# A graph network with residual layer norm on one core: where listed rows get their node numbers, their x and z rows, and how chunk additions are cut

## The chip, the core and the metric

One NeuronCore of a Trainium2 chip runs the whole kernel in one launch. Its engines are TensorE (PE), VectorE (DVE), ScalarE (ACT), GpSimd (POOL) and SyncE (SP). The metric is device time in microseconds (us); less is better.

## What is computed

There are 50,000 nodes with 128 features and 25,000 edges, sorted by target node. Four edge convolutions follow one another; each takes the features of an edge's source (all earlier outputs joined) and 16 edge features, and takes the mean at the target:

```python
def _edge_conv(x, src, dst, edge_attr, W, b, denom):
    msg = jnp.concatenate([x[src], edge_attr], axis=1) @ W + b
    s = jax.ops.segment_sum(msg, dst, num_segments=x.shape[0])
    return s / denom[:, None]
h = _edge_conv(x, src, dst, edge_attr, W0, b0, denom)
outputs = [h]
for W, b in ((W1, b1), (W2, b2), (W3, b3)):
    cat = jnp.concatenate(outputs, axis=1)
    outputs.append(_edge_conv(cat, src, dst, edge_attr, W, b, denom))
return _layernorm(x + outputs[-1])
```

The targets are drawn with a squared uniform number, so low node numbers have many edges.

## The kernel before

**Front.** Up to about 300 us POOL gathers x rows of all edges, PE sums them by target into UT in SBUF, and DVE makes tables of the edges by one-hot matmuls.

**Products.** Then 36 groups of 512 summed rows (18 steps of two) go through PE (products with M and WE), ACT (scaling into HS3, two buffers), SP (stores three parts of each row to part_rows) and POOL (L686, adds the fourth part as z to the node's row of x_and_z_of_nodes). While they run, DVE and PE make lists in `list_work(g)`, one piece for each group g: the edges whose source is itself a target (the first list, up to 70 blocks of 128), the edges among those that are needed once more (the second list), and their targets. `list_work(34)` calls `lists_done`, whose last step is eight calls in `unit_counts` (how many units, groups and blocks each list takes), and then sets `list_ready`.

**Rounds.** All engines wait for `list_ready` and read the counts into registers. POOL then runs this sequence, which is the order of everything behind the products:

- round 1: gathers (L710) of 128 rows of part_rows into 12 slots of G, which PE sums by one-hot matrices (OH, built by DVE) and DVE adds into UT (`add_first`)
- update 1: DVE scales the sums (`scale_rows`, L1769), POOL adds them to part_rows (L723) and waits for them to land
- round 2 and update 2: the same once more; round 3: the sums for the first list
- DVE takes the node numbers of the listed rows out of the sums in UT (L1832 to L1835, `final_ready`); each gathered row carries its number as a payload
- `gather_final` (L742): for each of the 58 blocks of listed rows a gather of x and z of 128 nodes into LZ, six pairs of slots in the place of EC. DVE scales the sums, adds z and x (`stats_batch`, L1786 and L1789), takes the statistics (L1794) in batches of ten blocks, and ACT normalizes them
- `last_rows` (L749): 58 scatters of the normalized rows to the output, once every chunk (below) is stored.

A unit is a run of these instructions inside nested branches; which units run depends on the counts (`nested`).

**Chunks.** All nodes, listed or not, also get the plain result layernorm(x + z): 30 chunks of 13 x 128 rows. SP loads x and z of a chunk (four and two buffers), DVE adds them in one instruction over 1664 columns (L1673), takes 13 statistics (L1658), and ACT normalizes and stores (L896). DVE's order puts 2 chunks into each of rounds 1 and 2, 7 behind the scaling of each update, 8 into round 3 and 4 among the last rows.

## Time and profile before

| | us |
|---|---|
| median of 3 runs (lowest to highest) | 989.87 (981.63 to 991.86) |
| the profiled execution | 988.91 |
| its span on the core | 987.1 |

The indirect transfers that POOL issues behind the products: 28 in round 1, 24 in update 1, 28 in round 2, 24 in update 2, 70 in round 3, 58 gathers of x and z, 58 scatters of the output.

In a row of a timeline the first number is the start in us from the span's start, the second the duration in us, then come engine, line, operation, output<-input by name, and in brackets the idle time of the engine before it and what ended it. The span is one execution; the median is taken over others.

### The profile page before, as it was taken

Reading aid. Unit: us, or ns where it says so; the run is one execution under the profiler, and the core shown is the slowest. Engines: PE = TensorE matmul, PEld = TensorE weight load, DVE = VectorE, ACT = ScalarE, POOL = GpSimd, SP = SyncE. Lnnn points to the kernel's source line nnn. Section 1 sums busy time; section 2 is a strip of 40 time slices with the busy share of each in tenths; the row PEclk is TensorE's granted clock in tenths of the full one; section 3 lists DMA queues with packets and bytes.
Section 4 is the critical chain, followed back from the end, with each engine's and each line's share of the span. In section 5 each row is a group of like instructions: output and inputs, shape, how many; then the busy total and the mean of one; then the engine's idle time right before and its main releaser. Section 6 shows DMA issues by size and latency. Waiting matters only on the chain.

```text
span 987.1 us, 13464 instructions
## 1 busy us (share of the span) xinstructions
PE 456.9 (46%) x2876; PEld 337.3 (34%) x2876; DVE 691.0 (70%) x2454; ACT 513.5 (52%) x1350; POOL 705.7 (71%) x652
## 2 busy tenths in 40 slices
PE   3456555767678889977825200540047550000000
PEld 1345553545455556644414100430035440000000
DVE  6888898777878976676667766867769973798000
ACT  7677774665667556665614065526466440367100
POOL 6677776777774677777747487748787774777775
PEclk9666556666768999999957555765577785555555
DMA  6799993999913568755677399959999972654111
GB/s 177 221 296 282 291 301 101 311 322 328 306 46 126 178 219 267 239 181 175 212 236 237 67 285 295 315 142 250 304 347 323 313 257 58 200 170 141 51 51 39
DMA packets 216937, 213.65 MB, mean 216 GB/s; under 512 B 18770, under 2 KB 198859, under 8 KB 216815
## 3 DMA queue, kind: packets, MB, share of 16 engines
q1 hardware_dynamic: 186159, 142.21, 46.8%
q0 software_dynamic: 26336, 44.55, 16.8%
q10 hardware_dynamic: 4320, 25.56, 6.3%
q8 instruction: 41, 0.67, 0.3%
q14 instruction: 81, 0.66, 0.2%
HBM read 116.84 MB, written 121.34 MB: 241 GB/s over the span
## 4 chain that ended last, share of the span: by engine, by line
POOL 29%; DVE 28%; issue 15%; DMA 11%; PE 11%; ACT 2%; DVEq 2%; POOLq 0%; ACTq 0%
POOL G L710 10%; POOL part_rows L723 8%; POOL out_rows L749 6%; DVE area L1096 5%; POOL x_and_z_of_nodes L686 3%; DMA G<-part_rows,s0r 2%; POOL EC L742 2%; PE hp L1988 2%; DMA area<-src_low_rows 2%; DMA AC<-src_low_rows 2%; PE segp L1988 2%; DMA x_and_z_of_nodes<-area,sum_rows 2%; DMA G<-part_rows,dsti 1%; DVE area L1303 1%; PE segp L1884 1%
## 5 line engine op out<-in xcount | busy, mean ns | idle before, releaser
L676 POOL DMA_INDIRECT G<-x_in,srci x196 | 210.0, 1072 | 78.0 <-issue 54.7
L686 POOL DMA_INDIRECT x_and_z_of_nodes<-area,sum_rows x140 | 141.6, 1011 | 57.9 <-issue 29.0
L896 ACT ACTIVATE area<-area,AC 128x128 f32<-128x128 f32 x299 | 117.5, 480 | 44.4 <-DVE AC L1680 44.4
L710 POOL DMA_INDIRECT G<-part_rows,s0r x70 | 80.8, 1154 | 23.6 <-issue 18.9
L835 ACT ACTIVATE UT<-segp,UT 128x1 f32 x168 | 43.9, 261 | 87.4 <-PE segp L1884 63.3
L868 ACT ACTIVATE area<-hp,zero,inv 128x512 f32<-128x512 f32 x72 | 53.7, 778 | 59.2 <-DMA x_and_z_of_nodes<-area,sum_rows 32.4
L1884 PE MATMUL segp<-SX,G 128*128 128x128 f32 x336 | 80.0, 426 | 4.3 <-ACT SX L811 3.3
L2121 PE MATMUL segp<-ZERO 128*128 128x390 f16 (+1 forms) x34 | 14.6, 431 | 144.5 <-DVE EC L1700 142.7
L742 POOL DMA_INDIRECT EC<-x_and_z_of_nodes,idx x58 | 61.4, 1059 | 27.9 <-issue 16.2
L1884 PEld LDWEIGHTS segp<-SX,G 128*128 128x128 f32 x336 | 72.8, 325 | 4.9 <-ACT SX L811 3.5
L889 ACT ACTIVATE AC<-AC,eps 128x13 f32<-128x13 f32 x30 | 9.2, 306 | 119.3 <-DVE AC L1666 115.2
L749 POOL DMA_INDIRECT out_rows<-UT,idx x58 | 57.1, 984 | 19.7 <-issue 19.7
L2127 PE MATMUL segp<-G,EC 128*128 128x130 f32 (+1 forms) x272 | 52.4, 353 | 31.9 <-DMA G<-part_rows,s0r 16.9
L1988 PE MATMUL hp<-LATE,UT 128*128 128x384 f32 x144 | 62.7, 519 | 0.0
L2127 PEld LDWEIGHTS segp<-G,EC 128*128 128x128 f32 x272 | 48.1, 259 | 40.7 <-DMA G<-part_rows,s0r 20.8
L1658 DVE BATCH_NORM_STATS2 AC<-area 128x6 f32<-128x128 f32 x299 | 60.1, 277 | 0.8
L807 ACT ACTIVATE SX<-iota,rel 128x128 f32<-128x128 f32 x196 | 60.4, 395 | 0.0
L1988 PE MATMUL segp<-LATE,UT 128*128 128x384 f32 x144 | 60.3, 501 | 0.0
L868 ACT ACTIVATE area<-segp,zero,inv 128x512 f32<-128x512 f32 x72 | 54.4, 779 | 10.9 <-PE segp L1988 9.6
L2127 PE MATMUL hp<-G,EC 128*128 128x130 f32 (+1 forms) x232 | 45.7, 359 | 28.2 <-DMA G<-part_rows,s0r 15.0
L723 POOL DMA_INDIRECT part_rows<-UT,nlo x24 | 43.3, 1804 | 19.9 <-DVE UT L1769 12.9
L723 POOL DMA_INDIRECT part_rows<-UT,shi x24 | 43.4, 1808 | 17.0 <-DVE UT L1769 10.0
(471 smaller groups left out, 1485.4 us busy)
## 6 DMA issues: line engine op xcount, KB each, us to landing
part_rows<-area SPq DMA_DIRECT2D x36, 768.0 KB
area<-x_and_z_of_nodes SPq DMA_DIRECT2D x30, 832.0 KB, 7.8
x_and_z_of_nodes<-ZERO SPq DMA_DIRECT2D x24, 1024.0 KB
x_and_z_of_nodes<-x_in SPq DMA_DIRECT2D x24, 1024.0 KB
area<-x_in SPq DMA_DIRECT2D x23, 832.0 KB, 7.6
out_rows<-area ACTq DMA_DIRECT2D x23, 832.0 KB, 5.2
LATE<-x_in SPq DMA_DIRECT2D x7, 832.0 KB, 7.5
out_rows<-LATE ACTq DMA_DIRECT2D x7, 832.0 KB, 7.7
```

The lines of the kernel that those rows point to most:

```text
L676: g.indirect_dma_start(G[:, slot, 0:D], None, x, bass.IndirectOffsetOnAxis(ap=srci[:, c:c + 1].bitcast(u32), axis=0), bounds_check=last_no ...
L686: g.indirect_dma_start(XZ2, bass.IndirectOffsetOnAxis(ap=sum_rows[:, c:c + 1], axis=0), HS3[:, q % 2, j, 3 * D:4 * D], None, bounds_check= ...
L710: g.indirect_dma_start(G[:, n % GS, 0:D], None, rows, bass.IndirectOffsetOnAxis(ap=take[k][:, n:n + 1], axis=0), bounds_check=last_part, o ...
L723: g.indirect_dma_start(TB3, bass.IndirectOffsetOnAxis(ap=l2_at[k - 1][:, b:b + 1], axis=0), own_row(b, w), None, bounds_check=last_part, o ...
L742: g.indirect_dma_start(LZ[:, 2 * r + w, :], None, XZ[0:N, :], bass.IndirectOffsetOnAxis(ap=node_u[:, b:b + 1], axis=0), bounds_check=last_ ...
L749: g.indirect_dma_start(out, bass.IndirectOffsetOnAxis(ap=node_u[:, b:b + 1], axis=0), own_row(b, W1), None, bounds_check=last_node, oob_is ...
L807: last = a.activation(FAR[:, j, :], iota[:, 0:P], ACT.Abs, bias=rel[:, c:c + 1], scale=-1.0)
L868: a.activation(HS3[:, b, j, :], PBANK[j][:, :], ACT.Identity, bias=zero1[:, 0:1], scale=inv[:, g * CG + j:g * CG + j + 1]).then_inc(s["p_a ...
L896: last = a.activation(XLS[b][:, k], XLS[b][:, k], ACT.Identity, bias=shift[:, b, r:r + 1], scale=rs[:, b, r:r + 1])
L1884: t.matmul(XBANK[k][:, at_:at_ + P], G[:, slot, 0:D], S[:, slot, :], start=True, stop=True).then_inc(s["summed"], 1)
L1988: t.matmul(PBANK[j][:, 0:3 * D], UT[:, (g * CG + j) * P:(g * CG + j + 1) * P], M[:, :], start=False, stop=True).then_inc(s["p_mm"], 1)
L2127: last = t.matmul(bank[:, bass.ds(at_, width)], OH[:, g % OHG, j, w * P:(w + 1) * P], G[:, slot, 0:width], start=False, stop=j == 1 and w ...
```

## The change

It has four parts.

**Node numbers.** They are now computed while the products run. `rank_places` (DVE, in `list_work(2)`) notes rank and node number of the first list's rows; `rank_build` (DVE) builds one-hot matrices for 10 chunks in `list_work(24)` to `(31)`, `rank_sums` (PE) multiplies them, 7 matmuls of 128 columns for each chunk, and `rank_nodes` (DVE) writes the numbers right behind `lists_done`. Six of the eight unit counts move to earlier places, the tables of units lose two entries, and each engine reads a count where it needs it, behind the first unit of a stage, instead of all ahead of round 1.

**Wide gathers.** The 58 gathers of x and z (`gather_wide`) get 58 places of their own in WIDE, the end of UT, and wait for no buffer. POOL issues them in block order 40 to 57, 30 to 39, ..., 0 to 9: 8 behind round 1, 2 behind update 1 (ahead of its wait for landing), 6 behind round 2, 2 behind update 2, 8 spread over round 3, and 32 behind it. This holds for short lists (`sizes < FAST`: both lists in their first units and at most 18 steps); otherwise the former order is kept in a branch of its own.

**Chunks.** They run from chunk 3 up to 29 and then 2, 1, 0. Three each go into rounds 1 and 2, seven into round 3, and the last three among the listed rows. The scatters of blocks 40 to 57 wait only for the first 27 chunks, those of lower blocks for the chunks that hold their nodes.

**Pieces.** A chunk's addition is four instructions over 4, 3, 3 and 3 rows of 128, each followed by its statistics.

```diff
+PIECES = ((0, 4), (4, 7), (7, 10), (10, LR))
-LROUND = (None, 2, 2, 8)
+LROUND = (None, 3, 3, 7)
+FPHASES = (0, 8, 10, 16, 18, 26)
+MBUILD = {24: (0, 1), 26: (2, 3), 27: (4,), 28: (5,), 29: (6,), 30: (7,), 31: (8, 9)}
+MSUM = {25: (0, 1), 27: (2, 3), 28: (4,), 29: (5,), 30: (6,), 31: (7,), 32: (8, 9)}
@@ POOL
-            n_e, n_l, n_q, n_s2, n_m, n_b = list_counts(e, (UNITS_R, UNITS_L, PAIRS, UNITS_S, UNITS_M, BLOCKS_M))
+            sizes = over_sizes(e)
...
+            def gather_wide(lo, hi):
+                for i in range(lo, hi):
+                    g.indirect_dma_start(WIDE[:, FORDER[i], :], None, XZ[0:N, :], bass.IndirectOffsetOnAxis(ap=node_u[:, FORDER[i]:FORDER[i] + 1], axis=0),
+                                         bounds_check=last_node, oob_is_err=False).then_inc(gat[FGROUP[i]], 16)
...
+            with e.If(sizes < FAST):
+                round_(1, UNITS_S, few, end=FEW_UNITS[1])
+                e.wait_ge(s["at_ready"], 1)
+                gather_wide(FPHASES[0], FPHASES[1])
+                update_rows(1, FPHASES[1:3], FEW_UNITS[2])
...
+                round_(3, UNITS_R, few, range(FPHASES[4], FPHASES[5]), FEW_UNITS[0])
+                gather_wide(FPHASES[5], FB)
+                for b in range(RING):
+                    e.wait_ge(st_o[b], 16 * len(range(b, LEARLY, RING)))
+                e.wait_ge(s["rest_out"], 16)
+                put_rows(OPEN_BLOCKS, FB)
@@ DVE
+            def rank_build(c):
+                b = c % 2
+                if c >= 2:
+                    e.wait_ge(s["tab_mm"], UNITS + c)
+                ones_by_pairs(RLO[:, b, :, :], RANK_LO, c, P)
+                if c:
+                    e.wait_ge(s["oh_built"], UNITS + 1 + c)
+                link(ones_by_pairs(RHOT[:, :, :], RANK_HI, c, MBLOCKS))
+                for w, value in enumerate((NODE_HI, NODE_LO)):
+                    last = v.tensor_tensor(in_twos(RVAL[:, b, :, w, :]), in_twos(RHOT[:, :, :]), spread_pairs(value, c, MBLOCKS), ALU.mult)
+                last.then_inc(s["oh_built"], 1)
...
-                unit_counts(((1, 0, 1, cf[:, 1:2]), (4, 0, 2, cf[:, 1:2]), (2, 3, 1, cf[:, 6:7]), (5, 3, 4, cf[:, 6:7]),
-                             (8, 5, 1, cf[:, 5:6]), (9, 5, 6, cf[:, 5:6]), (10, 7, 1, cf[:, 7:8]), (11, 7, 8, cf[:, 7:8])))
+                unit_counts(((10, 7, 1, cf[:, 7:8]), (11, 7, 8, cf[:, 7:8])))
...
-                lnk(v.tensor_tensor(XLS[b], XLS[b], ZL[:, c % ZRING, :], ALU.add))
+                for lo, hi in PIECES:
+                    own = XLS[b][:, lo * D:hi * D]
+                    lnk(v.tensor_tensor(own, own, ZL[:, c % ZRING, lo * D:hi * D], ALU.add))
+                    for r in range(lo, hi):
+                        last = v.bn_stats(stat[al, b, r, :], XLS[b][:, r * D:(r + 1) * D])
```

On POOL, between round 1 and round 2, this stood before (L710 gathers for a round, L723 adds to part_rows; the branches skip units that are not needed):

```order
L710 DMA G<-part_rows,dsti 128x128 x50
L106 UNCONDITIONAL_BRANCH
L723 DMA part_rows<-UT,nlo 76803x128 x20
L106 COMPARE_AND_BRANCH
L723 DMA part_rows<-UT,nlo 76803x128 x4
```

and this stands there now (L739 is a wide gather, TENSOR_LOAD and ISA read a count):

```order
L748 DMA G<-part_rows,dsti 128x128 x50
L123 UNCONDITIONAL_BRANCH
L739 DMA UT<-x_and_z_of_nodes,idx 128x256 x8
L764 DMA part_rows<-UT,nlo 76803x128 x20
L447 TENSOR_LOAD counts
L447 ISA x2
L447 TENSOR_LOAD counts
L447 ISA x2
L123 COMPARE_AND_BRANCH
L764 DMA part_rows<-UT,nlo 76803x128 x4
```

Eight wide gathers have come between the round and the update, and two reads of counts into the update.

On POOL, in the last units of round 3 and behind it, before:

```order
L710 DMA G<-part_rows,s0r 128x128 x60
L106 COMPARE_AND_BRANCH
L710 DMA G<-part_rows,s0r 128x128 x6
L106 COMPARE_AND_BRANCH
L710 DMA G<-part_rows,s0r 128x128 x4
...
L742 DMA EC<-x_and_z_of_nodes,idx 128x256 x58
...
L749 DMA out_rows<-UT,idx 50000x128 x58
```

and now:

```order
L739 DMA UT<-x_and_z_of_nodes,idx 128x256
L748 DMA G<-part_rows,s0r 128x128 x3
L447 TENSOR_LOAD counts
L447 ISA x2
L123 COMPARE_AND_BRANCH
L748 DMA G<-part_rows,s0r 128x128 x6
L123 COMPARE_AND_BRANCH
L748 DMA G<-part_rows,s0r 128x128 x4
L123 UNCONDITIONAL_BRANCH
L739 DMA UT<-x_and_z_of_nodes,idx 128x256 x32
L807 DMA out_rows<-UT,idx 50000x128 x58
```

Of the 58 gathers 32 are left behind the round, one in every seventh or eighth place stands inside it, and the other 18 are further ahead.

On DVE, a chunk before:

```order
L1673 TENSOR_TENSOR area<-area 128x1664
L1658 BN_STATS AC<-area 128x6 x13
L1662 TENSOR_TENSOR AC<-AC 128x13
```

and now:

```order
L1814 TENSOR_TENSOR area<-area 128x512
L1816 BN_STATS AC<-area 128x6 x4
L1814 TENSOR_TENSOR area<-area 128x384
L1816 BN_STATS AC<-area 128x6 x3
L1814 TENSOR_TENSOR area<-area 128x384
L1816 BN_STATS AC<-area 128x6 x3
L1814 TENSOR_TENSOR area<-area 128x384
L1816 BN_STATS AC<-area 128x6 x3
L1801 TENSOR_TENSOR AC<-AC 128x13
```

The same columns are added and the same 13 statistics taken, in turns.

## Rows read from the trace of the kernel before

**Rows 1.** The page: busy time of each engine; the chain by engine

```profile
PE 456.9 (46%) x2876; PEld 337.3 (34%) x2876; DVE 691.0 (70%) x2454; ACT 513.5 (52%) x1350; POOL 705.7 (71%) x652
...
POOL 29%; DVE 28%; issue 15%; DMA 11%; PE 11%; ACT 2%; DVEq 2%; POOLq 0%; ACTq 0%
```

**Rows 2.** Timeline of POOL: first indirect transfer of each stage, then the last (start, duration)

```profile
503.20 1.06 POOL L710 DMA_INDIRECT G<-part_rows,dsti  x1 [9.36 <-issue]
...
555.12 1.83 POOL L723 DMA_INDIRECT part_rows<-UT,nlo  x1 [12.86 <-DVE UT L1769]
...
609.24 1.86 POOL L710 DMA_INDIRECT G<-part_rows,previ  x1 [3.80 <-DMA part_rows<-UT,nlo]
...
659.09 1.82 POOL L723 DMA_INDIRECT part_rows<-UT,shi  x1 [10.01 <-DVE UT L1769]
...
712.05 1.07 POOL L710 DMA_INDIRECT G<-part_rows,s0r  x1 [2.55 <-DMA part_rows<-UT,shi]
...
824.39 0.99 POOL L742 DMA_INDIRECT EC<-x_and_z_of_nodes,idx  x1 [10.54 <-DVEq L1836]
...
905.49 1.02 POOL L749 DMA_INDIRECT out_rows<-UT,idx  x1 [2.29 <-issue]
...
978.94 0.98 POOL L749 DMA_INDIRECT out_rows<-UT,idx  x1 [0.31 <-issue]
```

**Rows 3.** The page, costliest groups: third-round gathers (count, busy, mean ns, idle before)

```profile
L710 POOL DMA_INDIRECT G<-part_rows,s0r x70 | 80.8, 1154 | 23.6 <-issue 18.9
```

**Rows 4.** Timelines, round 3: a chunk addition on DVE, two gathers on POOL

```profile
743.80 1.88 DVE L1673 TENSOR_TENSOR area<-area 128x1664 f32<-128x1664 f32 x1
...
743.29 1.00 POOL L710 DMA_INDIRECT G<-part_rows,s0r  x1 [0.30 <-issue]
...
744.59 1.96 POOL L710 DMA_INDIRECT G<-part_rows,s0r  x1 [0.30 <-PE hp L2127]
```

**Rows 5.** Timelines, update 1: row scaling on DVE, two adds to part_rows on POOL

```profile
554.15 3.70 DVE L1769 TENSOR_TENSOR UT<-UT,nhi 128x512 f32<-128x512 f32 x6
...
557.26 2.04 POOL L723 DMA_INDIRECT part_rows<-UT,nlo  x1 [0.31 <-issue]
...
559.60 1.55 POOL L723 DMA_INDIRECT part_rows<-UT,nlo  x1 [0.30 <-issue]
```

**Rows 6.** Timelines, end of lists: last unit count and round start (DVE); last products (ACT)

```profile
497.38 0.23 DVE L1391 SCALAR_TENSOR_TENSOR wlo<-unit_table,cf 128x9 f32<-128x9 f32 x1
...
497.65 0.15 DVE L1392 CAST counts<-cf 128x1 int32<-128x1 f32 x1
...
505.75 0.17 DVE L1698 COPY G<-SX 128x4 f32<-128x4 f32 x1 [4.71 <-issue]
...
492.74 1.44 ACT L868 ACTIVATE area<-segp,zero,inv 128x512 f32<-128x512 f32 x2
```

**Rows 7.** The page, DMA issues: product stores, chunk stores (count, size, us to landing)

```profile
part_rows<-area SPq DMA_DIRECT2D x36, 768.0 KB
...
out_rows<-area ACTq DMA_DIRECT2D x23, 832.0 KB, 5.2
```

**Rows 8.** Windows, late products: busy us of each engine (instructions), clock, DMA share, GB/s

```profile
430.00:482.00 52.00, 46.03 (x243) 27.33 (x244) 31.09 (x90) 32.71 (x49) 39.08 (x38) 0.90 0.55 187
```

**Rows 9.** Timeline of DVE, late products: one-hot columns of a list chunk

```profile
438.40 0.62 DVE L1096 TENSOR_TENSOR area<-iotah,low_pairs 128x896 bf16<-128x896 f16 x1
```

**Rows 10.** Timeline of DVE, last rows: batch statistics, chunk addition, next batch statistics

```profile
871.59 2.03 DVE L1794 BATCH_NORM_STATS2 area<-UT 128x6 f32<-128x128 f32 x10
...
874.65 1.95 DVE L1673 TENSOR_TENSOR area<-area 128x1664 f32<-128x1664 f32 x1
...
885.36 2.03 DVE L1794 BATCH_NORM_STATS2 area<-UT 128x6 f32<-128x128 f32 x10
```

**Rows 11.** Windows: between round 1 and update 1, and the first half of round 3

```profile
542.00:555.00 13.00, 5.34 (x26) 5.02 (x26) 5.85 (x19) 0.00 (x0) 0.26 (x1) 0.63 0.23 76
...
712.00:760.00 48.00, 26.02 (x126) 21.83 (x126) 38.42 (x162) 28.68 (x75) 38.21 (x33) 0.69 1.01 342
```

325 lines of the change are left out of this document (242 added, 83 removed).

## The prediction

> **What bounds the kernel now.** I read the page first, then the timeline of POOL from the end of the products to the end of the span, then DVE beside it. No engine is busy over 71% and the chain is shared out over all [rows 1], so shares decide nothing here; the stages do. Behind the products every stage is a run of indirect transfers on POOL. A gather takes 1.00 us and 0.30 us pass to the next [rows 4], so 1.30 us; an add to part_rows 1.55 [rows 5] and the same 0.30, so 1.85. Stage by stage, each end being the next start less the idle time in its brackets [rows 2]:
>
> - round 1: 503.20 to 542.26, 39.1 us for 28 gathers; 28 x 1.30 = 36.4, surplus 2.7
> - update 1: 555.12 to 605.44, 50.3 for 24; 24 x 1.85 = 44.4, surplus 5.9
> - round 2: 609.24 to 649.08, 39.8; surplus 3.4
> - update 2: 659.09 to 709.50, 50.4; surplus 6.0
> - round 3: 712.05 to 813.85, 101.8 for 70; 91.0, surplus 10.8 (mean 1154 ns for a plain 997 to 1000 [rows 3, 4])
> - gathers of x and z: 824.39 to 903.20, 78.8 for 58; 75.4, surplus 3.4
> - scatters: 905.49 to 979.92, then 7.2 us to the end of the span.
>
> So POOL is full inside the stages, and what is not its own rate is the idle time between them (12.9, 3.8, 10.0, 2.6, 10.5, 2.3 us) and a surplus of 32.2 us. The idle times of 12.9 and 10.0 are the landing of the last gathers, their sums and the scaling on DVE; 10.5 is the same plus the node numbers.
>
> **Where the surplus comes from.** The chunk addition on DVE runs from 743.80 to 745.68; the gather that was under way is not touched, the one that starts at 744.59 takes 1.96 instead of 1.00 and ends 0.87 behind the addition [rows 4]. So near its start a gather needs something that the addition holds. 32.2 us over 30 additions is 1.07 each. Short additions cost less: while DVE scaled rows in six instructions of 0.62 us (one merged row of 3.70), an update took 2.04 for 1.55 [rows 5], and the one ahead of it 1.83 [rows 2]: 0.77 us for six pieces, 0.13 each. The pieces of a chunk are 512 and 384 columns: 0.62 us, and 0.48 between that and the 1.88 us for 1664. A stall that begins anywhere in the 1.30 us grid grows with the square of the length, and (0.62² + 3 x 0.48²) / 1.88² = 0.30, or 0.3 us; four of the measured 0.13 make 0.5. I take 0.4, with 0 and 1.07 as the bounds.
>
> The Trainium skill (SBUF — State Buffer, "Who interferes with whom") says that `tensor_tensor` contends with GpSimd's reads only, and infers that descriptor generation needs only the write interface; by that reading alone the pieces would bring nothing, and the surplus would have another cause. The 1.96 us gather speaks against it. The same section has the first one in hold the port for its whole instruction, which is the third rival.
>
> **The change, term by term** (against the span of 987.1).
>
> 1. *Products and lists.* Six unit counts leave the tail. The last takes 497.38 to 497.80 [rows 6], with its link 0.46, so -2.8 us; seven reads of registers between `list_ready` (497.8) and the first gather (503.20) go as well. But round 1 also needs the last product rows stored: ACT ends them at 494.18 [rows 6], and a store of similar size lands 5.2 us behind its issue (832 KB, for 768 KB of products [rows 7]), so 499.4 and the start at about 499.9: -3.3 at best. Against it stands new work in the products: `rank_build` is one instruction like the 0.62 us one [rows 9] and three of half the columns at about 0.33, so 1.6 us, ten times 16 us, plus 4 us for `rank_places` and counts. DVE has 52.0 - 31.1 = 21 us free between 430 and 482 [rows 8], but most of it is waiting for PE in a loop that both must pass once a group, and PE, 46 us busy, gets 70 more matmuls (about 5 us). I take +3.8 for lateness, so +0.5 in all; bounds -3.3 and +12.
> 2. *Round 1.* A read of a count (+0.65: seven reads took at most the 5.4 us above, and DVE's eight took 4.71 idle [rows 6]), three chunks at 0.4: 36.4 + 1.2 + 0.65 = 38.3, -0.8.
> 3. *Between round 1 and update 1.* Eight wide gathers are 10.4 us in a gap of 12.9. The gap ends with DVE, which does not get slower (its addresses are taken over 64 columns instead of 196); 0. The DMA engines are 0.23 busy there [rows 11], so the transfers hinder nobody. The six behind round 2 are 7.8 us in 10.0; 0.
> 4. *Updates.* Surplus 0.8 + 7 x 0.4 = 3.6 instead of 5.9 and 6.0, two reads (+1.3) each: -1.0 and -1.1. The two wide gathers behind each (2.6 us) lie in the wait for landing, 3.8 and 2.6: 0.
> 5. *Round 2.* As round 1, 38.3 instead of 39.8: -1.5.
> 6. *Round 3.* 78 x 1.30 = 101.4, seven chunks 2.8, a read 0.65, other stalls 0.5: 105.4 instead of 101.8, +3.6. The DMA share there is 1.01 [rows 11]; the eight gathers add 1 MB, one chunk less takes 2.5 MB away.
> 7. *Behind round 3*, measured from its last gather (813.85): before 173.2 us to the end. Now 0.3 + 32 x 1.30 + 1.2 (three chunks) = 43.1, the waits 2.3, and the scatters with the end 81.6: 127.0, -46.2. DVE must keep up. It begins about 10 us behind the last gather; a batch with its pairs and a chunk take 885.36 - 871.59 = 13.8 us [rows 10], 5.3 of it the chunk, so six batches and three chunks 8.5 x 6 + 5.8 x 3 = 68 us, end 78, normalized by 83. POOL wants the last ten blocks at 45.4 + 48 x 1.29 = 107. The tightest is the batch 30 to 39: normalized at about 65, wanted at 45.4 + 18 x 1.29 = 68.6.
>
> Sum: 0.5 - 0.8 - 1.0 - 1.1 - 1.5 + 3.6 - 46.2 = -46.5. The span becomes 940.6, the time 940.6 + 1.8 (988.91 - 987.1) = 942.4. The profiled execution is 1.0 us under the median of the three, which I take in half: **943 us**, 4.7% less.
>
> **Rivals.**
> - *The pieces bring nothing* (what stalls POOL is the sum of the additions, not their length). 27 additions x 0.67 more: 961 us. For it: two updates under continuous scaling were slowed too; against it: 0.13 per piece.
> - *The products become late.* DVE and PE take turns in groups 24 to 31; 12 us instead of 0.5: 955 us. For it: PE 46 of 52 us busy, ACT waiting in between. Against it: DVE's free 21 us.
> - *A piece waits for the running gather.* DVE then loses some 0.5 us three more times a chunk; its tail gets 5 us longer, the batch 30 to 39 comes 2 us late: 945 us. The Trainium skill's rule of the held port, named above, is this rival; the addition of 743.80 began in the middle of a gather and was no longer than the others, which speaks against it.
> - *POOL does better still*: reads of counts hidden behind queued transfers (-4.5), pieces free of stalls (-8): 931 us.
> - *The fast order is not taken.* It needs both lists in their first units: round 3 gathered 70 blocks [rows 3], which is the limit of the new table, and 36 product stores are 18 steps [rows 7], its limit too; both hold. Otherwise the 58 gathers stay behind round 3 and only the pieces and -1.5 of term 5 are left: about 978.
> - *Slower than before*: the new builds turn DVE, PE and ACT from neighbours into one chain, since PE's group waits for DVE's builds and DVE's next build for PE's sums. One behind another, PE's 46.0 and DVE's 31.1 us between 430 and 482 [rows 8] with 20 and 5 new ones are 102 us instead of 52, and with half of ACT's 32.7 in it 118: +66, less the 3.8 in the sum, 1005 us. It decides where the stretch grows past 52 + 50 = 102 us. Against it: DVE builds a group ahead, so that PE would have to wait at every build.
>
> **How the numbers follow.** The sum as worked out 0.55 (its own range 935 to 950), pieces without effect 0.12, late products 0.15, waiting pieces 0.05, POOL better still 0.09, fast order not taken 0.02, the chain 0.02. The range takes in 931 and 961: **930 to 962**. About 1% is what a measurement of this kernel can tell from no change. Faster by over 1% (under 980) hold all but the last one, and I give the next to last, at 978, half: 0.96 with some rounding; within 1% 0.02; slower 0.02.
>
> **What would show each step.** In the new trace: wide gathers of 1.00 us in the two gaps, updates starting within 1 us of where the scaling is done; gathers and updates with few above 1.3 and 1.9 us while pieces of 0.48 us run on DVE; the start of round 1 at 500 to 508; 78 gathers in round 3 in about 105 us; no idle time of POOL between the wide gathers and the end but one of 2 to 3 us. It is wrong if POOL idles among the scatters (DVE or ACT late), if the start of round 1 is past 510, or if mean gather times stay at 1150 ns.

## The result

| | before | after |
|---|---|---|
| median of the runs shown, us | 990.87 (981.63 to 992.16) | 961.75 (959.47 to 962.24) |
| profiled execution, us | 988.91 | 961.59 |
| its span, us | 987.1 | 959.8 |

The ratio is 0.974, with a 95% interval of 0.970 to 0.977: the change makes the kernel 2.6% faster, where 4.7% was predicted. The predicted 943 us was 19 us too low; the measured median lies at the upper end of the range, 962, and the ratio of the runs taken side by side puts it a little past it (0.974 of 989.87 is 964).

The page of the changed kernel, parts 1 and 4 and two rows of part 5, answers to [rows 1] and [rows 3]:

```profile
PE 455.2 (47%) x2922; PEld 342.6 (36%) x2946; DVE 719.8 (75%) x2596; ACT 515.9 (54%) x1350; POOL 679.3 (71%) x652
...
DVE 43%; PE 12%; issue 12%; POOL 11%; DMA 11%; ACT 5%; DVEq 3%; ACTq 0%; SPq 0%; POOLq 0%
...
L716 POOL DMA_INDIRECT x_and_z_of_nodes<-area,sum_rows x140 | 141.2, 1009 | 69.2 <-ACT area L944 38.1
...
L748 POOL DMA_INDIRECT G<-part_rows,s0r x70 | 71.1, 1016 | 22.8 <-issue 18.0
```

Two things stand in these rows. A gather of round 3 now takes 1016 ns and not 1154: most of the stall is gone. And the chain that ended last runs through DVE for 43% of the span instead of 28% [rows 1]: the others now wait for DVE more than before.

The timeline of POOL in the changed kernel, the places that answer to [rows 2] (start, duration, idle time ahead in brackets):

```profile
501.68 0.98 POOL L716 DMA_INDIRECT x_and_z_of_nodes<-area,sum_rows  x1 [0.30 <-ACT area L944]
...
509.09 1.05 POOL L748 DMA_INDIRECT G<-part_rows,dsti  x1 [6.43 <-issue]
...
544.67 1.01 POOL L748 DMA_INDIRECT G<-part_rows,dsti  x1 [0.30 <-issue]
545.99 1.00 POOL L739 DMA_INDIRECT UT<-x_and_z_of_nodes,idx  x1 [0.30 <-issue]
...
566.00 1.83 POOL L764 DMA_INDIRECT part_rows<-UT,nlo  x1 [9.71 <-DVE UT L1914]
...
617.26 0.99 POOL L748 DMA_INDIRECT G<-part_rows,previ  x1 [2.95 <-DMA part_rows<-UT,nlo]
...
652.91 0.99 POOL L748 DMA_INDIRECT G<-part_rows,previ  x1 [0.30 <-issue]
...
673.16 1.83 POOL L764 DMA_INDIRECT part_rows<-UT,shi  x1 [11.29 <-DVE UT L1914]
...
723.82 1.12 POOL L748 DMA_INDIRECT G<-part_rows,s0r  x1 [1.78 <-DMA part_rows<-UT,shi]
...
825.40 0.99 POOL L748 DMA_INDIRECT G<-part_rows,s0r  x1 [0.30 <-PE segp L2336]
...
895.86 1.01 POOL L807 DMA_INDIRECT out_rows<-UT,idx  x1 [3.61 <-ACT UT L995]
...
946.12 0.98 POOL L807 DMA_INDIRECT out_rows<-UT,idx  x1 [0.30 <-issue]
```

L748 gathers of the rounds, L739 wide gathers, L764 updates, L807 scatters to `out`. The wide gathers stand where the change puts them and cost 1.00 us each. But the update behind them starts at 566.00, which is 20.3 us behind the end of round 1 (545.68); before it was 12.9. Laid beside the prediction's terms (us; each stage from its first start to its last end, a gap from end to start, wide gathers in it):

| term | before | after | change | predicted | off by |
|---|---|---|---|---|---|
| 1 start of round 1 | 503.20 | 509.09 | +5.9 | +0.5 | +5.4 |
| 2 round 1 | 39.1 | 36.6 | -2.5 | -0.8 | -1.7 |
| 3 gap ahead of update 1 | 12.9 | 20.3 | +7.4 | 0 | +7.4 |
| 3 gap ahead of update 2 | 10.0 | 19.3 | +9.3 | 0 | +9.3 |
| 4 updates 1 and 2 | 50.3 and 50.4 | 45.6 and 46.2 | -8.9 | -2.1 | -6.8 |
| 4 gaps behind them | 3.8 and 2.6 | 5.7 and 4.5 | +3.8 | 0 | +3.8 |
| 5 round 2 | 39.8 | 36.6 | -3.2 | -1.5 | -1.7 |
| 6 round 3 | 101.8 | 102.6 | +0.8 | +3.6 | -2.8 |
| 7 from the last round gather to the end | 173.2 | 133.4 | -39.8 | -46.2 | +6.4 |
| sum | | | -27.2 | -46.5 | +19.3 |

The terms of POOL's own stages (2, 4, 5 and 6) came out 13 us better than predicted. The others came out 32 us worse: the start, the gaps, and the stretch behind round 3. The experiments take these apart.

### The profile page after: what moved, and what is told of

Same layout as the page of the kernel before. It is cut to its first block, busy times and chain, and to the rows that moved or that the text cites. A ratio compares the mean times of both kernels' runs of the same rounds, so it can differ in the third digit from the quotient of the medians.

```text
span 959.8 us, 13751 instructions
## 1 busy us (share of the span) xinstructions
PE 455.2 (47%) x2922; PEld 342.6 (36%) x2946; DVE 719.8 (75%) x2596; ACT 515.9 (54%) x1350; POOL 679.3 (71%) x652
## 4 chain that ended last, share of the span: by engine, by line
DVE 43%; PE 12%; issue 12%; POOL 11%; DMA 11%; ACT 5%; DVEq 3%; ACTq 0%; SPq 0%; POOLq 0%
DVE area L1192 7%; DMA G<-part_rows,s0r 4%; POOL part_rows L764 4%; POOL G L748 3%; DVE AC L1816 3%; POOL out_rows L807 3%; PE hp L2187 2%; PE segp L2187 2%; DMA area<-x_and_z_of_nodes 2%; DVE area L1814 2%; DMA area<-src_low_rows 2%; DMA AC<-src_low_rows 2%; ACT LATE L973 2%; ACT area L973 2%; DVE UT L1928 2%
## 5 line engine op out<-in xcount | busy, mean ns | idle before, releaser
L748 POOL DMA_INDIRECT G<-part_rows,s0r x70 | 71.1, 1016 | 22.8 <-issue 18.0
L2083 PE MATMUL segp<-SX,G 128*128 128x128 f32 x336 | 76.9, 414 | 5.0 <-ACT SX L887 3.3
L2083 PEld LDWEIGHTS segp<-SX,G 128*128 128x128 f32 x336 | 70.2, 314 | 5.6 <-ACT SX L887 3.6
L807 POOL DMA_INDIRECT out_rows<-UT,idx x58 | 57.3, 988 | 21.0 <-issue 17.1
L739 POOL DMA_INDIRECT UT<-x_and_z_of_nodes,idx x58 | 59.2, 1021 | 17.7 <-issue 17.7
L1816 DVE BATCH_NORM_STATS2 AC<-area 128x6 f32<-128x128 f32 x299 | 66.9, 282 | 3.1
L2187 PE MATMUL hp<-LATE,UT 128*128 128x384 f32 x144 | 62.2, 515 | 11.6 <-issue 8.0
L1814 DVE TENSOR_TENSOR area<-area 128x512 f32<-128x512 f32 (+1 forms) x92 | 53.0, 576 | 18.8 <-DMA area<-x_and_z_of_nodes 18.8
L2336 PE MATMUL segp<-G,EC 128*128 128x130 f32 (+1 forms) x272 | 55.2, 368 | 18.7 <-DMA G<-part_rows,s0r 16.5
L944 ACT ACTIVATE area<-segp,zero,inv 128x512 f32<-128x512 f32 x72 | 55.0, 778 | 14.1 <-PE segp L2187 12.2
L2336 PEld LDWEIGHTS segp<-G,EC 128*128 128x128 f32 x272 | 53.6, 281 | 23.4 <-DMA G<-part_rows,s0r 19.7
L2330 PEld LDWEIGHTS segp<-ZERO 128*128 128x128 f16 x34 | 4.2, 123 | 158.2 <-DVE EC L1844 156.7
L764 POOL DMA_INDIRECT part_rows<-UT,shi x24 | 39.1, 1631 | 18.3 <-DVE UT L1914 11.3
```

The lines of the kernel that those rows point to most:

```text
L748: g.indirect_dma_start(G[:, n % GS, 0:D], None, rows, bass.IndirectOffsetOnAxis(ap=take[k][:, n:n + 1], axis=0), bounds_check=last_part, o ...
L764: g.indirect_dma_start(TB3, bass.IndirectOffsetOnAxis(ap=l2_at[k - 1][:, b:b + 1], axis=0), own_row(b, w), None, bounds_check=last_part, o ...
L807: g.indirect_dma_start(out, bass.IndirectOffsetOnAxis(ap=node_u[:, b:b + 1], axis=0), own_row(b, W1), None, bounds_check=last_node, oob_is ...
L944: a.activation(HS3[:, b, j, :], PBANK[j][:, :], ACT.Identity, bias=zero1[:, 0:1], scale=inv[:, g * CG + j:g * CG + j + 1]).then_inc(s["p_a ...
L1814: lnk(v.tensor_tensor(own, own, ZL[:, c % ZRING, lo * D:hi * D], ALU.add))
L1816: last = v.bn_stats(stat[al, b, r, :], XLS[b][:, r * D:(r + 1) * D])
```

## The experiments

### What the pieces are worth

**p1_before_pieces**, the kernel before with the pieces alone:

```diff
-                lnk(v.tensor_tensor(XLS[b], XLS[b], ZL[:, c % ZRING, :], ALU.add))
+                for lo, hi in PIECES:
+                    own = XLS[b][:, lo * D:hi * D]
+                    lnk(v.tensor_tensor(own, own, ZL[:, c % ZRING, lo * D:hi * D], ALU.add))
+                    for r in range(lo, hi):
+                        last = v.bn_stats(stat[al, b, r, :], XLS[b][:, r * D:(r + 1) * D])
+                lnk(last)
```

> The kernel before with one part of the change alone: the chunk addition in four pieces, each followed by the statistics of its rows. Theory 1 (long additions hold up POOL): the updates shrink from 50.3 to about 46 us, the rounds 1 and 2 by 2.5 to 3 us each, the mean gather of round 3 from 1154 to about 1020 ns (70 x 0.13 = 9 us), the last 58 gathers by 2 us; the gaps in front of the updates stay near 13 and 10 us, since DVE has waits to spare there. Together about -24 us: 967 us. By the 0.67 us per chunk of the prediction it would be -20: 971 us. Theory 2 (the pieces bring nothing, the new order made POOL quicker): 988 to 992 us.

Measured: 980.37 us, ratio 0.991 (0.988 to 0.994). **p2_whole**, the changed kernel with one piece:

```diff
-PIECES = ((0, 4), (4, 7), (7, 10), (10, LR))
+PIECES = ((0, LR),)
```

> The changed kernel with its chunk additions whole again (one piece of 13 rows). Theory 1: POOL loses again what the pieces gave, 4 us per update, 2.5 us per round, 9 to 10 us in round 3, 1 to 2 us behind it; each chunk is 0.5 us shorter on DVE, which gives back at most 3 us in the gaps: 980 to 986 us. Theory 2 (order, not pieces): 962 us.

Measured: 974.36 us, ratio 0.985 (0.980 to 0.990), against 0.974 with four pieces. So the pieces are worth 8 to 9 us in the one kernel and 11 to 13 in the other, where theory 1 had expected 24 (967 us) and 18 to 24 (980 to 986 us): its direction is shown, theory 2 falls in both, and its sizes were missed. Rounds 1 and 2 and both updates of p1 shrank nearly as expected, 2.2 to 2.6 and 4.6 us each. Page and groups of instructions of p1 (rounds and updates):

```profile
L711 POOL DMA_INDIRECT G<-part_rows,s0r x70 | 72.0, 1029 | 30.8 <-issue 18.6 <-DMA part_rows<-UT,shi 5.3 <-PE hp L2130 4.0
...
L724 POOL DMA_INDIRECT part_rows<-UT,nlo x24 | 38.7, 1612 | 20.1 <-DVE UT L1772 13.1 <-issue 7.0
```

A round-3 gather takes 1029 ns (before 1154 [rows 3]), an update's put 1612 instead of 1804. But the idle time went up: POOL waits 5.3 us for the landing of the second update and not 2.55 [rows 2], and 4.0 us for PE instead of 1.5. Round 3 as a whole got only 4.2 us shorter (97.6 for 101.8), though its gathers are busy 8.8 us less, and the wait behind it for the node numbers grew from 10.54 to 14.35 us. In p1's trace the stages are 18 us shorter in all, the waits between them 9 us longer, and round 1 starts 2.6 us later. The timeline of p1 at the starts of rounds 2 and 3:

```profile
606.87 1.08 POOL L711 DMA_INDIRECT G<-part_rows,previ  x1 [5.52 <-DMA part_rows<-UT,nlo]
...
705.78 1.08 POOL L711 DMA_INDIRECT G<-part_rows,s0r  x1 [5.25 <-DMA part_rows<-UT,shi]
```

An update issued in 45.7 us instead of 50.3 is waited for longer behind its last add: of 4.6 us, 1.7 and 2.7 are given back in the wait. From the first add to the first gather of the next round it is still shorter, 51.2 and 51.1 us instead of 54.1 and 53.0. There are no wide gathers in this kernel, so the growth of these two gaps in the changed kernel, from 3.8 and 2.6 us to 5.7 and 4.5, isn't theirs either.

**p12_two_pieces** stands on p8 (below) and has two pieces:

```diff
-PIECES = ((0, 4), (4, 7), (7, 10), (10, LR))
+PIECES = ((0, 7), (7, LR))
```

> The same version (946.29 us) with two pieces per chunk addition (7 and 6 rows, about 1.05 and 0.92 us) instead of four (0.48 to 0.62 us). An update takes 45.5 us with four pieces, 49.5 to 51.9 with one; rounds 1 and 2 take 36.6 to 36.9 and 39.1 to 42.3. Theory N (a stall grows with the square of a piece's length, as the prediction had it): (1.05 x 1.05 + 0.92 x 0.92) / (1.88 x 1.88) = 0.55 of the whole addition's stall, updates about 48 us, rounds 38.0, 956 us. Theory O (only what a piece is longer than the grid of about 1 us for one issue stalls POOL): updates within 0.7 us of 45.5, 946 us.

Measured: 955.15 us, ratio 0.965 (0.960 to 0.970), updates of 48.1 and 49.0 us, rounds of 37.1 and 37.3. Theory O falls: the updates are 2.7 us longer than p8's in both places. Theory N's 956 us and its 48 us for an update are met; its 38.0 for a round is not, and 2.3 us of this trace's longer span come from a later start of round 1 (509.49 for 507.23), which the pieces don't explain. The same two groups of instructions in p2 (one piece), p12 (two), and p8 (four):

```profile
L748 POOL DMA_INDIRECT G<-part_rows,s0r x70 | 77.8, 1111 | 21.3 <-issue 18.3 <-PE segp L2336 2.1 <-PE hp L2336 0.9
L764 POOL DMA_INDIRECT part_rows<-UT,shi x24 | 44.9, 1870 | 11.2 <-issue 7.0 <-DVE UT L1914 4.2
```

```profile
L748 POOL DMA_INDIRECT G<-part_rows,s0r x70 | 72.9, 1041 | 22.4 <-issue 18.9 <-PE segp L2324 1.5 <-DMA part_rows<-UT,shi 1.3
L764 POOL DMA_INDIRECT part_rows<-UT,shi x24 | 42.0, 1749 | 11.4 <-issue 7.0 <-DVE UT L1907 4.4
```

```profile
L748 POOL DMA_INDIRECT G<-part_rows,s0r x70 | 71.0, 1015 | 22.9 <-issue 18.9 <-DMA part_rows<-UT,shi 1.8 <-PE hp L2324 1.5
L764 POOL DMA_INDIRECT part_rows<-UT,shi x24 | 39.3, 1637 | 11.7 <-issue 7.0 <-DVE UT L1907 4.7
```

1111, 1041 and 1015 ns for a gather, 1870, 1749 and 1637 for a put. The surplus of all stages over 1.30 and 1.85 us per transfer, reckoned as in the prediction over 30 chunks, is 34.4 us with one piece, 14.6 with two, 5.3 with four: 1.15, 0.49 and 0.18 us a chunk, if all of the surplus is put down to the chunks.

### The gaps ahead of the updates

DVE's timeline around the end of round 1, changed kernel. L1814 is the first addition of the round's first chunk, L1857 and L1858 are the last sums of the round, L1995 the first instruction behind it:

```profile
521.27 0.69 DVE L1814 TENSOR_TENSOR area<-area 128x512 f32<-128x512 f32 x1 [6.49 <-DMA area<-x_and_z_of_nodes]
...
557.31 0.28 DVE L1857 TENSOR_TENSOR UT<-UT,segp 128x130 f32 x1
557.51 0.42 DVE L1858 COPY UT<-segp 128x260 f32 x1
563.28 0.27 DVE L1995 TENSOR_TENSOR nhi<-UT,rela 128x64 f32<-128x64 f32 x1 [5.35 <-issue]
```

and the same place before:

```profile
548.36 0.29 DVE L1713 TENSOR_TENSOR UT<-UT,segp 128x130 f32 x1
548.57 0.42 DVE L1714 COPY UT<-segp 128x260 f32 x1
551.94 0.52 DVE L1822 TENSOR_TENSOR nhi<-UT,rela 128x196 f32<-128x196 f32 x1 [2.95 <-issue]
```

Two parts: DVE's last sum ends 12.2 us behind the last gather (557.93 - 545.68) and no longer 6.7 (548.99 - 542.25), +5.5; and then nothing runs on it for 5.35 instead of 2.95 us, +2.4. Addresses over 64 columns instead of 196 and the rest give 0.5 back (2.7 us from the first of them to the update instead of 3.2). Behind round 2 it is 13.1 instead of 6.3 and 5.16 instead of 2.72. DVE's waits show why it is late. First the changed kernel, 512 to 560 us, then the kernel before, 505 to 550:

```profile
DVE area L1814 <- DMA area<-x_and_z_of_nodes: 6.5, 1, 6.5
DVE G L1842 <- PE segp L2336: 0.7, 1, 0.7
```

```profile
DVE UT L1713 <- PE hp L2127: 5.2, 2, 3.8
...
DVE UT L1713 <- PE segp L2127: 4.6, 3, 2.6
```

Before, DVE waited 9.8 us for PE in this stretch, 5.2 of them before the last gather ended and 4.6 behind it, so it was at the gathers' heels. Now it waits for PE 0.7 us.

The first row of the timeline holds a second reason. DVE stood still for 6.49 us until the first chunk was loaded, and began it 12.2 us into the round (521.27 - 509.09); before, it waited 2.19 us and began 7.55 us in (510.75). All traces with three chunks of four pieces agree: the last sum comes 36.1 to 36.8 us behind the start of the first chunk, and how late it is behind the last gather follows from when that chunk began.

| kernel (three chunks) | first chunk begins, us into round 1 | last sum behind the last gather, us | gap ahead of update 1, us |
|---|---|---|---|
| p5 | 9.4 | 9.5 | 17.0 |
| p6 | 10.9 | 11.0 | 18.7 |
| p4 | 12.2 | 11.6 | 20.0 |
| changed kernel | 12.2 | 12.2 | 20.3 |
| p7 | 12.3 | 12.2 | 17.3 |

p7's gap is shorter because DVE stands still for less time behind its last sum, as shown below. So in round 1 the late first chunk adds to what the third one costs. No run changes the load alone and keeps three chunks; p5 and p6 moved it along with other things. With two chunks a round DVE has room again: p10 has its first chunk 2.5 us earlier in the round than p8 (9.7 for 12.2) and the same last sum (7.8 us).

**p3_two_chunks** takes the third chunk out of rounds 1 and 2 and puts both into round 3:

```diff
-LROUND = (None, 3, 3, 7)
+LROUND = (None, 2, 2, 9)
```

> The changed kernel with two chunks in rounds 1 and 2 as before (2, 2, 9 instead of 3, 3, 7). Theory A (the third chunk, put shortly before a round's end, makes DVE late with its last sums): DVE's last addition of a round comes 5.5 us (round 1) and 6.8 us (round 2) earlier, the gaps in front of the updates shrink from 20.3 and 19.3 us to about 15 and 13, round 3 stays near 103 us: 950 us. Theory B (the wide gathers behind the rounds hold up the landing of the last rows or the port): the gaps stay within 1 us of 20.3 and 19.3, 962 us.

Measured: 957.40 us, ratio 0.969 (0.965 to 0.973). The gaps are 12.8 (544.62 to 557.41) and 13.7 us (645.21 to 658.95). That is theory A, for its 15 and 13 us; theory B's 20.3 and 19.3 fall. But its 950 us were missed by 7. DVE's last sums come 7.4 and 8.8 us behind the last gather, so the third chunk accounts for 4.8 of the 5.5 us and 4.4 of the 6.8, and its idle time behind them shrinks by 2.7 and 1.2 us. Of the 9.3 us by which the second gap had grown 3.7 are still there; no run takes them apart.

```profile
557.41 1.83 POOL L764 DMA_INDIRECT part_rows<-UT,nlo  x1 [2.21 <-DVE UT L1914]
...
658.95 1.83 POOL L764 DMA_INDIRECT part_rows<-UT,shi  x1 [5.86 <-DVE UT L1914]
...
878.47 1.04 POOL L807 DMA_INDIRECT out_rows<-UT,idx  x1 [0.30 <-issue]
...
889.56 1.01 POOL L807 DMA_INDIRECT out_rows<-UT,idx  x1 [10.05 <-ACT UT L995]
```

The wide gathers are still there, so by themselves they don't set the gap. The last row shows why a first scatter 13.3 us earlier (855.83 for 869.13) became a span only 6.3 us shorter and a median 4.4 lower: POOL now waits 10.05 us for the batch 30 to 39 (3.61 in the changed kernel). Taking a chunk out of a round doesn't take it off DVE.

**p4_early_reads** has DVE read its five counts once, ahead of round 1, and leaves out the reads at the rounds' ends:

```diff
-                count, groups = list_counts(e, counted)
+                count, groups = counted
...
-                n_m, = list_counts(e, (UNITS_M,))
...
+            n_s2, n_g2, n_m, n_e, n_g = list_counts(e, (UNITS_S, GROUPS_S, UNITS_M, UNITS_R, GROUPS))
```

> The changed kernel, but DVE reads its five counts once, in front of round 1, as the kernel before did. Theory C (the 5.35 and 5.16 us without a releaser on DVE at the rounds' ends are longer than the 2.95 and 2.72 of before because of the two reads): they shrink to about 3 us, both gaps by 2.4 us, and the reads in front of round 1 are hidden in DVE's wait of 6.5 us for its first chunk: 957 us. Theory D (it is the branch and the fetching of instructions behind it): idle times unchanged, 962 us.

Measured: 961.10 us, ratio 0.972 (0.969 to 0.976), no difference from the changed kernel. DVE's idle time behind round 1 is 5.74 us:

```profile
560.54 0.27 DVE L1995 TENSOR_TENSOR nhi<-UT,rela 128x64 f32<-128x64 f32 x1 [5.74 <-issue]
```

Theory C falls: the reads are not what takes the time. The DMA queues give a hint of what does. Changed kernel, 557.9 to 563.3 us, then before, 549 to 552:

```profile
DMA packets 191, 0.87 MB, mean 160 GB/s; under 512 B 45, under 2 KB 45, under 8 KB 189
...
q10 hardware_dynamic: 111, 0.63, 28.7%
q0 software_dynamic: 73, 0.19, 9.4%
q8 instruction: 1, 0.02, 1.1%
...
q14 instruction: 1, 0.01, 0.4%
```

```profile
DMA packets 1, 0.01 MB, mean 3 GB/s; under 512 B 0, under 2 KB 0, under 8 KB 0
...
q14 instruction: 1, 0.01, 1.0%
```

In both there is a packet or two of instructions. In the one they share the engines with 111 packets of q10, the store of the third chunk, and 73 of q0, the last of the eight wide gathers; in the other they are alone. The idle times beside the rate in them:

| kernel | behind round 1: us idle, GB/s | behind round 2 |
|---|---|---|
| before | 2.95, 3 | 2.72, 3 |
| p8 (two chunks) | 2.60, 109 | 4.08, 96 |
| p3 (two chunks) | 2.62, 109 | 4.01, 86 |
| p7 (no wide gathers there) | 2.44, 66 | 3.60, 131 |
| p2 (one piece) | 4.90, 270 | 2.63, 60 |
| changed kernel | 5.35, 160 | 5.16, 205 |
| p4 | 5.74, 230 | 5.50, 265 |
| p5 | 4.75, 243 | 5.09, 225 |
| p6 | 5.00, 169 | 5.23, 164 |
| p1 | 2.61, 9 | 2.58, 17 |
| p9 | 2.74, 111 | 3.98, 70 |
| p10 | 2.56, 109 | 4.02, 99 |
| p11 | 2.62, 105 | 4.08, 62 |
| p12 | 2.74, 114 | 3.20, 49 |

Up to 131 GB/s it is 2.4 to 4.1 us, from 160 on 4.75 to 5.74. Below 131 the rate doesn't order them: the kernels with two chunks stand still for 2.6 to 2.7 us at 105 to 114 GB/s behind round 1, and all but one of them for 4.0 to 4.1 at 62 to 99 behind round 2. Four traces make a square for round 1. With neither the third chunk's store nor wide gathers it is 2.95 us (before), with the gathers alone 2.62 (p3), with the store alone 2.44 (p7, below), with both 5.35. So neither alone lengthens it there. Behind round 2 the changed kernel has next to no wide gathers left in this stretch, but the store and the load of a chunk. That the fetch of instructions waits behind the data is likely and not proved: no run changed the traffic alone, and the traces don't say whose instructions the packets carry. The Trainium skill (Runtime: NRT & Kernel Launch, "Instruction fetch mechanics") has a taken branch whose target is not in the engine's window force a DMA fetch before execution goes on; the packets in the idle time agree as far as they go. What it costs beside other traffic isn't stated there.

**p7_all_behind** moves all 58 wide gathers behind round 3:

```diff
-FPHASES = (0, 8, 10, 16, 18, 26)
+FPHASES = (0, 0, 0, 0, 0, 0)
```

> The changed kernel with all 58 wide gathers behind round 3 (none behind rounds 1 and 2, the updates, or in round 3). Theory K (POOL's issue is what they cost, and in the gaps they are free): rounds and gaps as in the changed kernel (36.6, 20.3, 45.6 us ...), small gaps behind the updates unchanged at 5.7 and 4.5 us, since they are landings; round 3 10.4 us shorter, the stretch of wide gathers 33.8 us longer, the idle 3.6 us among the scatters gone: 961.75 - 10.4 + 33.8 - 3.6 = 981 us. Theory B again (wide gathers hold up the landings and the gaps): gaps shorter by several us, 970 to 975 us.

Measured: 980.52 us, ratio 0.992 (0.989 to 0.994), for 981 expected. The total is theory K's, its parts are not: both gaps together are 4.5 us shorter than it had them, and a round 3 that is 1.6 us longer, a start 0.8 us later and smaller terms made up for that. The timeline of POOL:

```profile
563.92 1.83 POOL L764 DMA_INDIRECT part_rows<-UT,nlo  x1 [17.35 <-DVE UT L1914]
...
615.17 1.08 POOL L748 DMA_INDIRECT G<-part_rows,previ  x1 [5.49 <-DMA part_rows<-UT,nlo]
...
670.52 1.82 POOL L764 DMA_INDIRECT part_rows<-UT,shi  x1 [17.79 <-DVE UT L1914]
...
721.56 1.08 POOL L748 DMA_INDIRECT G<-part_rows,s0r  x1 [5.24 <-DMA part_rows<-UT,shi]
```

Gaps of 17.3 and 17.8 us without a single wide gather in them, and landings of 5.5 and 5.2 us: the wide gathers cost 3.0 and 1.5 us there, as much as DVE's idle time in the table above differs (2.9 and 1.6). That is little, and it is not nothing. Their early place is worth 18.8 us in all.

### The start of round 1

**p6_no_ranks**:

```diff
-MBUILD = {24: (0, 1), 26: (2, 3), 27: (4,), 28: (5,), 29: (6,), 30: (7,), 31: (8, 9)}
-MSUM = {25: (0, 1), 27: (2, 3), 28: (4,), 29: (5,), 30: (6,), 31: (7,), 32: (8, 9)}
+MBUILD = {}
+MSUM = {}
...
-                    rank_places()
...
-                link(v.tensor_scalar(wlo[:, 0:FB], XB[:, 0:FB], 256.0, None, ALU.mult))
-                link(v.tensor_tensor(wlo[:, 0:FB], wlo[:, 0:FB], XB[:, MBLOCKS:MBLOCKS + FB], ALU.add))
+                link(v.tensor_scalar(wlo[:, 0:FB], iota[:, 0:FB], float(P), None, ALU.mult))
+                link(v.tensor_scalar(wlo[:, 0:FB], wlo[:, 0:FB], iotap[:, 0:1], None, ALU.add))
```

> The changed kernel without the node numbers' sums: the 10 builds on DVE, their 70 matmuls on PE and the preparation are left out, and the node numbers are block x 128 + partition instead, so other rows of x and z are gathered and written. Theory H (this work makes the products late): the last product scatter is issued about 5 us earlier than 501 to 502, round 1 starts at about 503 instead of 507 to 509.5, and all stages behind it follow: 955 us. Theory I (the lateness comes from the unit counts and the other moved list steps, or is the spread between runs): round 1 within 1.5 us of 508, 961 us.

Measured: 955.23 us, ratio 0.967 (0.965 to 0.969). Timeline of POOL, last product scatter and start of round 1:

```profile
497.16 0.98 POOL L716 DMA_INDIRECT x_and_z_of_nodes<-area,sum_rows  x1 [0.31 <-ACT area L944]
502.04 1.06 POOL L748 DMA_INDIRECT G<-part_rows,dsti  x1 [3.90 <-DMA part_rows<-area]
```

This kernel gathers and writes the rows of other nodes, and is used for its time alone. Theory H: the last product is out 4.5 us earlier than at 501.68, and round 1 starts at 502.04. In nine traces with this work and the same order of branches it starts at 506.6 to 509.9, in the mean 508.3; in the two without any of the change in this part (before, p1) at 503.20 and 505.78. So the work costs 6.3 us, what else moved saves about 2.4 (the two traces without it are 2.6 us apart), and of the table's +5.9 about 2 are spread between executions. What round 1 waits for is not the products, though, but the end of DVE's lists. Timeline of DVE, last unit count of the changed kernel:

```profile
507.79 0.15 DVE L1528 CAST counts<-cf 128x1 int32<-128x1 f32 x1
```

The first gather starts 1.15 us behind the end of this instruction, in all nine traces. Before, and in p1, it starts 5.40 us behind it (497.80 to 503.20), with the reads of the counts in between. So the reads saved 4.25 us, and the lists end 10.1 us later than before. In p6 they end at 499.42, 7.8 us earlier than in the mean of the nine, and there the landing of the last product rows is what ends the wait: that bound hides 1.5 us of what the work costs. It also explains the late first chunk: POOL begins sooner behind the lists, while the loads of the chunks still wait for DVE's last conversions behind them (L1212, to 512.11).

In the changed kernel the builds take 9.2 + 7.0 = 16.2 us of DVE (groups of instructions, 430 to 503 us):

```profile
L1192 DVE TENSOR_TENSOR area<-iotah,area 128x896 f16<-128x896 f16 (+1 forms) x20 | 9.2, 501 | 0.1
L1505 DVE TENSOR_TENSOR area<-area 128x448 f16<-128x448 f16 x20 | 7.0, 389 | 0.3
```

### Behind the last scatter

The span ends 12.7 us behind the last scatter's end (946.12 + 0.98 to 959.8), before 7.2. **p5_fast_last** exchanges POOL's two branches, so that the taken one is last in the program and no jump over the other follows it (the diff only moves the block `with e.If(sizes > FAST - 1)` ahead of `with e.If(sizes < FAST)`).

> The changed kernel with POOL's two branches exchanged: the one that this input takes stands last in POOL's program. In four traces with the new branch the span ends 12.7 to 12.9 us behind the last scatter, in two without it 7.2. Theory F (POOL leaves the branch by a jump over the other one and must fetch instructions for its end): the end comes 7.2 us behind the last scatter, and the jump, now ahead of round 1, lies beside the wait for the last product rows: 956 us. Theory G (the jump costs the same ahead of round 1, where nothing hides it): 7.2 us at the end, round 1 5 us later, 961 us. Theory G2 (the 12.7 us are the landing of the last scatters): 12.7 us again.

Measured: 958.85 us, ratio 0.971 (0.969 to 0.974), profiled span 952.9. Timeline of POOL, start of round 1 and last scatter:

```profile
508.21 1.05 POOL L748 DMA_INDIRECT G<-part_rows,dsti  x1 [7.93 <-issue]
...
941.77 0.98 POOL L807 DMA_INDIRECT out_rows<-UT,idx  x1 [0.30 <-issue]
```

The end comes 10.15 us behind the last scatter (10.17 in p11, which has the same order of branches; 12.7 to 13.1 in the ten traces with the branches the other way round), and the two instruction packets ("q14 instruction: 2, 0.02, 0.3%" among the DMA queues between 944 and 960 us) that the changed kernel shows there are gone. So 2.6 of the 5.5 us are the jump. In front they come back in full: round 1 starts 3.74 us behind the last unit count instead of 1.15. But DVE is then less late, as the table of first chunks shows, and the gap ahead of update 1 falls to 17.0 us. The other 2.9 us at the end have no cause that was found. None of the three theories met the 10.15; G2 (all of it landing) is out, since the scatters land 2.3 us behind their issue in both. In the median p5 is 2.9 us below the changed kernel, and their ratios, 0.971 (0.969 to 0.974) and 0.974 (0.970 to 0.977), overlap.

### A version without the faults

**p8_two_interleaved** takes the two chunks of p3 and orders the tail so that each late chunk stands right ahead of the batch that has to wait for its store. On DVE (ACT has the same order, one step behind):

```diff
-                chunk(LEARLY)
-                shift_batch(*ts[opened - 1])
-                for c in range(LEARLY + 1, LCH):
-                    chunk(c)
-                for t, lo, n in ts[opened:]:
+                for t, lo, n in ts:
                     fast_batch(t, lo, n)
-                    if t > opened:
+                    if t and not 0 <= t - opened < LAFTER:
                         shift_batch(*ts[t - 1])
+                    if 0 <= t + 1 - opened < LAFTER:
+                        chunk(LEARLY + t + 1 - opened)
+                        shift_batch(*ts[t])
```

> The changed kernel with two chunks in rounds 1 and 2 (2, 2, 9), and with the three late chunks each ahead of the batch that may be written only after it (on DVE and ACT: batches 50 and 40, chunk, batch 30, chunk, batch 20, chunk, batches 10 and 0) instead of all three ahead of batch 30. With two chunks alone POOL waited 10.05 us among the scatters for batch 30 to 39. Theory J (only the order of DVE's and ACT's work makes POOL wait): batch 30 to 39 comes two chunks (12 us) earlier, no wait over 1 us among the scatters, 957.4 - 10.05 = 947 us. Theory L (DVE's whole work binds): the wait moves to the next batches, 955 to 957 us.

Measured: 946.29 us, ratio 0.960 (0.956 to 0.963), for 947 expected: theory J. The gaps are 13.1 and 12.6 us, and among the scatters POOL never waits over 0.31 us. The last one starts at 927.44, and the span still ends 13.0 us behind its end.

Three further steps from there. **p9_chunk_places** has the second chunk of rounds 1 and 2 at step 7:

```diff
+LPLACE[1] = LPLACE[2] = [3, 7]
```

> The version with two chunks in rounds 1 and 2 and the interleaved tail (946.29 us), with the second chunk of these rounds at DVE's step 7 instead of 9. Theory A again (what is left of the gaps, 13.1 and 12.6 us, is DVE catching up behind a late chunk; it was 12.9 and 10.0 before): both gaps shrink by 1 to 3 us to about 11, 942 us. Rival (landing, sums and the fetching of instructions alone set them): gaps within 0.7 us of 13.1 and 12.6, 946 us.

Measured: 944.98 us, ratio 0.958 (0.955 to 0.961); gaps of 12.8 and 13.0 us. Theory A's 942 us and gaps near 11 are missed, its rival's 946 and 13 are met: this move alone, with two chunks a round, changes nothing that can be told. **p10_casts_first**:

```diff
                     lists_done()
+                elif g == PACK_AT + 9:
                     row_limits()
                     rank_nodes()
```

> The same version (946.29 us), with row limits and node numbers behind the last four conversions of the edge table on DVE instead of ahead of them; the loads of the first chunks wait for these. Theory M (DVE's wait of 5.8 us for its first chunk carries over to the end of the kernel): the loads start about 2.7 us earlier, the first chunk begins as much earlier, but since POOL and not DVE now sets the end, the time changes by less than 1 us: 945 to 946 us. Rival (DVE is still the bound everywhere): 943.5 us.

Measured: 945.74 us, ratio 0.958 (0.956 to 0.961). DVE's wait for its first chunk fell from 5.81 to 3.05 us and the time stayed, as theory M has it. **p11_all_edits** has both and POOL's exchanged branches.

> The same version with both of these edits and with POOL's taken branch last. From the exchange of the branches alone 2.5 us came at the end (10.15 us behind the last scatter instead of 12.7) and at most 1.5 us went ahead of round 1. Expected: gaps near 11 us, 10.2 us at the end: 940 us. Rival (the gains overlap): 943 us or more.

Measured: 943.75 us, ratio 0.955 (0.952 to 0.958). The 940 us were missed, its rival's 943 or more is met: the end is 10.2 us behind the last scatter and the first gap 10.9, but round 1 starts at 510.16, the latest of all, round 3 takes 105.2 us instead of 102.7, with waits of 1.0 and 1.6 us for PE, and the second gap is 13.5. p8 to p11 can't be told from each other; all four are clearly faster than the changed kernel.

## Why the prediction was wrong

- **What bounds the kernel.** Right for POOL inside the stages, 1.30 and 1.85 us a transfer. It failed to ask how much room DVE had: 5.2 us of waiting for PE in round 1 before the last gather ended, and a chunk more costs 5.8 us (521.27 to 527.1) with the sums queued behind it.
- **Pieces.** The mechanism was right (p1, p2, p12), and so was the stall before, 1.07 us a chunk (1.15 in p2). Four pieces leave 0.18 and not 0.4. Over the 27 chunks of the rounds and updates that is 0.22 x 27 = 5.9 of the 13 us by which terms 2, 4, 5 and 6 came out better; seven reads of counts at 0.65, 4.6 us, are the next part, and the allowance for other stalls, 0.8 in each update and 0.5 in round 3, most of the rest. But a shorter stage isn't a shorter kernel: the waits for landing behind both updates grew by 3.8 us. The term that has "0" for the landing was priced with the old 3.8 and 2.6 us, though these were measured behind a slower POOL.
- **Term 1** was off by 5.4 us in this trace, and by about 3.3 with the mean starts of 508.3 and 504.5. The sum's +3.8 for lateness should have been +6.3 (p6); its -3.3 is about -2.4 by p1, p6 and before. It had the wrong thing last: it took the storing of the products for what round 1 waits for, and it was the end of DVE's lists, 10.1 us later than before. The builds measured 16.2 us, as reckoned, and 39% of that became lateness; that DVE's builds and not PE's 70 matmuls did it is argued, since p6 takes out both. The rival "products late" named the kind, with 12 us; in size the measured start lies between it and the sum.
- **Term 3** is the step that failed, by 16.7 us. "The gap ends with DVE, which does not get slower" held for the address instructions, which it argued from, and not for DVE as a whole: the third chunk (`LROUND` 3 instead of 2) stood in the diff and was priced only as a stall of POOL, 0.4 us. DVE's last sums came 5.5 and 6.8 us later, of which two chunks a round take back 4.8 and 4.4 (p3), in round 1 together with a first chunk that was loaded late. Behind the sums DVE stood still 2.4 us longer each time, while the DMA engines carried the third chunk's store, in the first gap beside wide gathers and in the second beside the load of a chunk; that this slows its fetch of instructions is likely and not proved. "The transfers hinder nobody" was judged by a DMA share of 0.23 from the kernel before; in the changed kernel the wide gathers cost 3.0 and 1.5 us there (p7) and not 0.
- **Reads of counts.** Priced at 0.65 us each on POOL; nothing is to be seen of them there (every pause in the stages stays 0.30 us), and on DVE p4 found nothing either.
- **Term 7.** The batch 30 to 39 was forecast 3.6 us ahead of POOL's demand. It came 68.7 us behind the last round gather instead of 65, POOL was there at 66.1 instead of 68.6, and 3.6 us of idle time were the result; in p8, with two chunks and another order, they are gone. The 5.5 us at the very end were not thought of: the change lets POOL leave a branch with another one behind it, which is 2.6 of them (p5). The 2.3 us wait ahead of the scatters, which the sum kept, did not come.
- **The signs and the rivals.** "Faster" was right, and the sign "POOL idles among the scatters" came true. No rival named what happened, which was that DVE became the bound in rounds 1 and 2. The first rival's 961 us lies on the measured time by luck: its reason, that the pieces bring nothing, is refuted by p1, p2 and p12. The 978 us of the rival without the fast order doesn't follow from its two terms, 18 us for the pieces and 1.5, which give about 970.

With two chunks a round and the tail's order mended, the changed kernel takes 946.29 us, 3 us from the predicted 943, and that nearness is luck too. In p8's trace the rounds and updates come out 12 us better than predicted and everything around them 13 us worse: the start by 3.5, the gaps by 2.8, the waits for landing by 3.9 and the stretch behind round 3 by 3.0.

## What to carry to other kernels

Before you price an instruction as "hidden", write down for each stage how long its engine waits there now; work put in beyond that waiting time is late in full, and everything queued behind it too. When the bound engine is made faster, look at what it used to wait for least (here DVE's sums and the load of its first chunk, DMA landings, the batches of the tail): that is the next bound, and it takes back part of the gain at once. If a piece of work only frees the next consumer, put it right ahead of that consumer and not with its like.
